# Warming TensorE by single fp32 products, and a down projection with standing weights for six of eight experts

## The chip, the core and the metric

One core of a Trainium2 chip runs the kernel. The metric is the device time of one execution in microseconds (us), the median of several runs. Its engines are TensorE (PE: products and transposes; PEld is its weight loading), VectorE (DVE), ScalarE (ACT), GpSimd (POOL) and SyncE (SP). Matrix products write PSUM, in eight banks; DMAs move data between SBUF and DRAM. Engines wait for each other by semaphores. PE's clock has two levels, 1.2 and 2.4 GHz; the profile gives the granted share.

## What is computed

A block on x (8, 16, 16, 128), so 2048 tokens of 128 channels, fp32: a linear attention with a residual, then a mixture of eight experts with a residual.

```python
x = x + conv_ref(_ln_c(x), w_qkv, q_gamma, q_beta, k_gamma, k_beta)   # heads of 16, q (k^T v) / n
t = _to_tokens(x)
t = t + ffn_ref(_ln_t(t), gate_w, gate_b, w1, b1, w2, b2)
...
# in ffn_ref: 8 experts, 2 per token, hidden 512
cap = int(CF * T / NE)                          # 307
probs = softmax(xf @ gate_w.T + gate_b)
topw, topi = top_k(probs, TOPK)
...
sel_w, sel_idx = top_k(wm.T, cap)               # each expert takes its 307 best tokens
xg = xf[sel_idx]
h = gelu(einsum('ecd,edh->ech', xg, w1) + b1[:, None, :], approximate=False)
out = einsum('ech,ehd->ecd', h, w2) + b2[:, None, :]
weighted = out * sel_w[..., None]
of = zeros((T, D)).at[sel_idx.reshape(-1)].add(weighted.reshape(-1, D))
```

## The kernel before, in words

Each engine has its own program, written out by hand in the order in which it runs; `wait_ge` and `then_inc` on named semaphores tie them together. There are four parts.

1. *Attention, 0 to 45 us.* The eight images go through a pipeline of steps over PE, ACT, DVE and POOL. SP loads x and the weights: after x come `gate_bias`, `b1_rows`, `w1_sb`, `w2_sb` and `b2_sb` (the biases b2 of all experts on every partition), then zeros are written to `parts`.
2. *Routing and thresholds, 45 to 76 us.* DVE computes the softmax and the two choices, and finds each expert's threshold, its 307th best weight, in nine rounds. In a round DVE compares (L729, `hits`), PE counts with 16 products (L1008, `ps_cnt`), DVE picks the digit (L743, L746). PE has time over in each round. It fills it with products on zeros, whose result nobody reads: `keep_warm` (L877) issues `times` bf16 products of `width` columns. There are 20 of 512 columns before the first round, 6 of 256 after each, 6 of 512 after the last and 10 of 512 after the running sums.
3. *Token lists, 76 to 90 us.* Of one-hot matrices PE makes the list of tokens of each expert (L1034 to L1054). POOL gathers the tokens' rows from `table` in DRAM by indirect DMAs: for each expert two of 128 rows (L436, `gather`), and for each pair of experts one with both tails of 51 rows (L441).
4. *Experts, 90 to 150 us.* 307 tokens are the chunks 128, 128 and 51. In the loop over e PE does
   - `up(e)`: four hidden blocks of 128, each w1 as weights and 307 tokens moving (L1072), into the banks `ps_h`;
   - `tokens_in(e + 1)`: three transposes of the gathered rows (L1066) into `ps_x`;
   - `down(e)`: three chunks (L1088), in each four products with the hidden values of 128 or 51 tokens as weights and w2 moving, 128 columns. They go by turns into the two banks `ps_ys`, so chunk n waits until chunk n - 2 is out (`y_ready`).

   A product in fp32 is two passes of PE, a transpose is one. ACT computes the gelu of each block with the bias b1 (L568), and copies `xgT` for experts 0 and 1 (L556). DVE copies the other `xgT` (L813), multiplies b2 by the tokens' weights ahead of time (`weigh_bias`, L825 and L827, into `wb2`) and takes each chunk out of PSUM by one instruction (L837, `tokens_out`): the product by the token's weight plus the weighted bias.

POOL scatters the rows to `parts` in DRAM (`put(e)`: one indirect DMA for each chunk of 128, L463, and one for the tails of a pair, L471; experts 6 and 7 have one each). All its transfers are one queue. The numbers of `GATHERS_AFTER` set it: ten gathers, put(0), three gathers (for expert 4 and the tails of 5), put(1), four gathers (5 and 6), put(2), three gathers (tails of 6 and 7, then 7), then put(3) to put(7). When the early puts are done SP loads the first half of `parts`, after put(7) the second; DVE adds both to the residual (L867, L871) and SP writes the result.

## Time and profile before

| | |
|---|---|
| median of 3 runs | 164.46 us (164.29 to 164.65) |
| profiled execution: its time | 163.72 us |
| its span, first to last instruction | 162.0 us |
| PE busy | 125.0 us (77%), 863 products or passes |
| PEld busy | 95.7 us (59%) |
| DVE busy | 86.7 us (54%), 324 instructions |
| ACT busy | 52.6 us (32%), 140 |
| POOL busy | 71.7 us (44%), 118 |
| down projection (L1088) | 192 passes, 26.7 us |
| up projection (L1072) | 64 passes, 22.8 us |
| `keep_warm` (L880) | 100 products, 21.2 us |
| instruction loads | 7 packets, 0.11 MB, 0.3% of the DMA engines |

Busy time is what an engine's instructions cover; a share of it doesn't say what sets the end. A row of the timeline gives the start in us from the span's beginning, the length, and in brackets how long the engine stood idle before and for whom. "issue" there names nobody.

### The profile page before, as it was taken

The numbers are of one execution on the slowest core, as the hardware profiler recorded it, in microseconds if no ns is written. First come the engines' busy times: TensorE is split into PE (matmuls) and PEld (weight loads), VectorE is DVE, ScalarE is ACT, GpSimd is POOL, SyncE is SP. The second block draws the span as 40 slices with busy tenths as digits, with TensorE's granted clock in tenths as the row PEclk, the third lists the DMA queues.
The fourth block names the chain that finished last, engine by engine and source line by source line (L and its number), as shares of the span: only waits on it lengthen the run. The fifth ranks groups of instructions, "written<-read, shape, count | busy, mean of one in ns | idle before, by whom it ended". The sixth has DMA issues, their size and how long they took to land.

```text
span 162.0 us, 2490 instructions
## 1 busy us (share of the span) xinstructions
PE 125.0 (77%) x863; PEld 95.7 (59%) x863; DVE 86.7 (54%) x324; ACT 52.6 (32%) x140; POOL 71.7 (44%) x118
## 2 busy tenths in 40 slices
PE   6899999998696564769985799983899799994000
PEld 3377999998642443545574468862668578873000
DVE  1567789766777888777863204321143234334442
ACT  3399777661289400000000242240040441450000
POOL 7405365456482060200048765777377244356100
PEclk9999999999959999999965569999569999999655
DMA  4679999300000008100001111112111010116497
GB/s 113 166 163 397 302 311 417 144 0 4 0 2 2 0 4 268 42 4 0 0 9 50 55 55 34 53 51 62 44 38 53 32 34 16 36 41 189 124 303 201
DMA packets 15596, 15.46 MB, mean 95 GB/s; under 512 B 1816, under 2 KB 12224, under 8 KB 15584
## 3 DMA queue, kind: packets, MB, share of 16 engines
q1 hardware_dynamic: 14240, 12.45, 24.7%
q0 software_dynamic: 1344, 2.86, 6.0%
q8 instruction: 7, 0.11, 0.3%
q14 instruction: 5, 0.04, 0.1%
HBM read 9.67 MB, written 5.64 MB: 94 GB/s over the span
## 4 chain that ended last, share of the span: by engine, by line
PE 48%; issue 26%; ACT 9%; DMA 7%; POOL 3%; SPq 2%; DVE 2%; POOLq 0%; another core or an unknown queue 0%; DVEq 0%
PE bank L1072 14%; PE bank L1088 14%; PE bank L903 4%; ACT rows L551 4%; DMA xb<-parts 3%; PE bank L930 2%; DMA vecs<-in_L_conv_k_beta_dram 2%; PE bank L943 2%; DMA parts<-y_tail,tail_rows 2%; PE bank L933 2%; PE bank L898 2%; PE bank L1066 2%; PE bank L916 1%; PE bank L960 1%; POOL parts L463 1%
## 5 line engine op out<-in xcount | busy, mean ns | idle before, releaser
L1088 PE MATMUL bank<-w_sb,hid 128*128 128x128 f32 (+1 forms) x192 | 26.7, 289 | 5.0 <-issue 4.8
L568 ACT ACTIVATE hid<-bank,b1T 128x307 f32<-128x307 f32 x32 | 16.3, 516 | 37.3 <-PE bank L1072 36.2
L1088 PEld LDWEIGHTS bank<-w_sb,hid 128*128 128x128 f32 (+1 forms) x192 | 22.7, 172 | 7.6 <-issue 5.5
L436 POOL DMA_INDIRECT kv<-table,index x16 | 16.5, 1032 | 20.5 <-DVE index L807 15.9
L463 POOL DMA_INDIRECT parts<-q_work,kv x16 | 15.9, 992 | 18.6 <-DVE q_work L837 10.8
L1072 PE MATMUL bank<-xgT,w_sb 128*128 128x307 f32 x64 | 22.8, 508 | 0.6 <-ACT xgT L556 0.6
L880 PE MATMUL bank<-warm_rhs 128*128 128x256 bf16 (+1 forms) x100 | 21.2, 356 | 1.4 <-POOL warm_rhs L355 1.4
L1072 PEld LDWEIGHTS bank<-xgT,w_sb 128*128 128x128 f32 x64 | 13.6, 224 | 6.8 <-issue 4.3
L837 DVE SCALAR_TENSOR_TENSOR q_work<-bank,kv,wb 128x128 f32<-128x128 f32 x16 | 5.6, 351 | 21.1 <-PE bank L1088 16.4
L1008 PE MATMUL bank<-hits,ones 128*128 128x56 bf16 (+1 forms) x144 | 7.8, 199 | 9.3 <-DVE hits L729 9.2
L880 PEld LDWEIGHTS bank<-warm_rhs 128*128 128x128 bf16 x100 | 9.5, 104 | 7.4 <-issue 2.7
L1008 PEld LDWEIGHTS bank<-hits,ones 128*128 128x128 bf16 x144 | 6.0, 97 | 12.7 <-DVE hits L729 9.7
L556 ACT ACTIVATE xgT<-bank 128x307 f32<-128x307 f32 x2 | 0.9, 426 | 36.1 <-issue 36.0
L415 POOL TENSOR_TENSOR att<-att,xb 128x256 f32<-128x256 f32 x8 | 5.8, 726 | 12.9 <-DVE xb L644 12.9
L813 DVE COPY xgT<-bank 128x307 f32<-128x307 f32 x6 | 2.9, 478 | 12.4 <-issue 12.4
L903 PE MATMUL bank<-w_c,xT 128*128 128x256 f32 x32 | 8.4, 386 | 0.3 <-ACT kv L538 0.3
L407 POOL TENSOR_TENSOR ksq<-kv,kq_rstd 128x256 f32<-128x256 f32 x8 | 5.0, 620 | 6.3 <-DVE kq_rstd L649 6.3
L903 PEld LDWEIGHTS bank<-w_c,xT 128*128 128x128 f32 x32 | 5.9, 190 | 1.9 <-ACT kv L538 1.1
L1034 PE MATMUL bank<-oh_tok,oh_maj 128*64 128x24 f16 (+1 forms) x48 | 6.0, 279 | 1.3 <-DVE oh_maj L785 1.3
L1034 PEld LDWEIGHTS bank<-oh_tok,oh_maj 128*64 128x64 f16 (+1 forms) x48 | 5.5, 195 | 1.9 <-DVE oh_maj L785 1.9
L1066 PEld LDWEIGHTS bank<-ident,kv 128*128 128x128 f32 (+1 forms) x24 | 3.7, 157 | 4.9 <-issue 3.9
L1066 PE MATMUL bank<-ident,kv 128*128 128x128 f32 (+1 forms) x24 | 5.2, 298 | 1.4 <-DMA kv<-table,index 1.4
(194 smaller groups left out, 235.6 us busy)
## 6 DMA issues: line engine op xcount, KB each, us to landing
w_sb<-in_L_ffn_w_dram SPq DMA_DIRECT2D x1, 2048.0 KB, 10.9
parts<-zeros SPq DMA_DIRECT2D x4, 512.0 KB, 7.2
table<-rows SPq DMA_DIRECT2D x1, 1152.0 KB, 5.4
x_sb<-parts SPq DMA_DIRECT2D x4, 256.0 KB, 3.9
xb<-parts SPq DMA_DIRECT2D x4, 256.0 KB, 3.8
out_dram<-att SPq DMA_DIRECT2D x4, 256.0 KB, 2.8
x_sb<-in_x_dram SPq DMA_DIRECT2D x1, 512.0 KB, 4.5
b_sb<-in_L_ffn_b_dram SPq DMA_DIRECT2D x1, 512.0 KB, 18.0
```

The costliest lines, as they stand in the source:

```text
L415: pool.tensor_tensor(x1[:, img(b), :], att[:, img(b), :], xb[:, img(b), :], ALU.add).then_inc(x1_ready, 1)
L436: pool.indirect_dma_start(out=xg_chunk(e, c), out_offset=None, in_=table, in_offset=bass.IndirectOffsetOnAxis(ap=index[:, index_at(e, c):i ...
L463: pool.indirect_dma_start(out=parts, out_offset=bass.IndirectOffsetOnAxis(ap=xg_rows[:, e // 2, at, C + E + e:C + E + e + 1], axis=0), in_ ...
L551: act.activation(rows[:, t, 0:C], x1[:, t, :], ACT.Identity, bias=shift2[:, t:t + 1], scale=rstd2[:, t:t + 1]).then_inc(x2_ready, 1)
L568: act.activation(hid[:, e % 2, c, :], ps_h[c][:, 0:CAP], ACT.Gelu, bias=b1T[:, e * HC + c:e * HC + c + 1]).then_inc(h_ready, 1)
L880: pe.matmul(bank[:, 0:width], warm_rhs[:, 0:P], warm_rhs[:, 0:width], start=True, stop=True)
L903: ins = pe.matmul(ps_kv[:, i * 2 * C:(i + 1) * 2 * C], xT[:, t * P:(t + 1) * P], w_c[:, C:3 * C], start=True, stop=True)
L1008: ins = pe.matmul(ps_cnt[:, 0:n * E], ones16[:, :], hits[:, r % 2, 0:n, t, :], start=(t == 0), stop=(t == NT - 1))
L1034: ins = pe.matmul(ps_grids[g][0:MAJ * m, 0:CM * m], majors[:, :, t], minors[:, :, t], start=(t == 0), stop=(t == NT - 1))
L1066: ins = pe.transpose(ps_x[:, at:at + n], xg_chunk(e, c)[:, 0:C], ident[own, own])
L1072: pe.matmul(ps_h[c][:, 0:CAP], w1_sb[:, e, c * P:(c + 1) * P], xgT[:, e % 2, :], start=True, stop=True).then_inc(h_done, 1)
L1088: ins = pe.matmul(ps_ys[(NC * e + k) % 2][y_at:y_at + n, 0:C], hid[:, e % 2, c, at:at + n], w2_sb[:, e, c, :], start=(c == 0), stop=(c == ...
```

## The change

Two parts, and what hangs on them.

*Warming.* A new `keep_warm_long` multiplies the fp32 tile `zeros` by itself. Before the rounds there are 6 of 512 columns instead of 20 bf16 ones, after each round 1 of 384 instead of 6 of 256, after the last 1 of 512 instead of 6, after the running sums 2 instead of 10. The other calls of `keep_warm` stay.

*Down projection.* `TURNED` is 6. For experts 0 to 5 the weights w2 stand and the 307 tokens move: four products into bank 5 give the output with channels on the partitions (`down_turned`). ACT takes it out and adds b2 as a bias per partition (`yT`). PE turns it back by three products on the identity into bank 6 (`turn`; a chunk that lands on partitions 64 and up is an ordinary product, not a transpose), one expert later: `turn(e - 1)` stands between `tokens_in(e + 1)` and `down(e)`. DVE multiplies by the token's weight, both chunks of 128 in one instruction and the tail in a second (`turned_out`). For experts 6 and 7 all stays as it was. The rows of b2 are loaded and turned with those of b1; only two experts' b2 is spread over the partitions.

```diff
+    TURNED = E - 2
...
+        yT = sb("yT", [C, 2, CAP])
...
+        ps_yT = banks[5]
+        ps_turned = banks[6]
...
+        def written(e, c):
+            if e < TURNED:
+                return 2 * e + (1 if c < LAST else 2)
+            return 2 * TURNED + NC * (e - TURNED) + c + 1
...
+            sp.dma_start(b_rows[0:E * HC, :], b1.rearrange("e (c p) -> (e c) p", p=P)).then_inc(b_in, 16)
+            sp.dma_start(b_rows[E * HC:E * HC + E, :], b2).then_inc(b_in, 16)
...
-                         b2.rearrange("e c -> (e c)").partition_broadcast(P)).then_inc(b_in, 16)
+                         b2[TURNED:E, :].rearrange("e c -> (e c)").partition_broadcast(P)).then_inc(b_in, 16)
...
-                    pool.wait_ge(y_ready, NC * e + c + 1)
+                    pool.wait_ge(y_ready, written(e, c))
...
+                if e < TURNED:
+                    act.wait_ge(yT_done, e + 1)
+                    if e >= 2:
+                        act.wait_ge(y_done, e - 1)
+                    act.activation(yT[:, e % 2, :], ps_yT[:, 0:CAP], ACT.Identity,
+                                   bias=bT[:, E * HC + e:E * HC + e + 1]).then_inc(yT_ready, 1)
...
+            def turned_out(e):
+                at, last = e % 2 * HALF, CHUNKS[LAST][1]
+                slot_of, to = tail_of(e)
+                dve.wait_ge(y_done, e + 1)
+                dve.tensor_tensor(y[:, e, :, :], ps_turned[:, 0:LAST * C].rearrange("p (n c) -> p n c", c=C),
+                                  main_weight(e), ALU.mult).then_inc(y_ready, 1)
+                dve.tensor_scalar(y_tail[to:to + last, slot_of, :], ps_turned[at:at + last, LAST * C:NC * C],
+                                  xg_chunk(e, LAST)[:, C + e:C + e + 1], None, ALU.mult).then_inc(y_ready, 1)
...
-            weigh_bias(0)
-            tokens_out(0)
-            weigh_bias(1)
+            tail_to(0)
             for e in range(1, E):
+                tail_to(e)
+                if e >= TURNED:
+                    weigh_bias(e)
                 if e + 1 < E:
                     tokens_in(e + 1)
-                tokens_out(e)
-                if e + 1 < E:
-                    weigh_bias(e + 1)
+                if e - 1 < TURNED:
+                    turned_out(e - 1)
+                if e >= TURNED:
+                    tokens_out(e)
...
+            def keep_warm_long(bank, times, width=512):
+                for _ in range(times):
+                    pe.matmul(bank[:, 0:width], zeros[:, 0:P], zeros[:, 0:width], start=True, stop=True)
...
-            keep_warm(ps_kv, 20)
+            pe.wait_ge(zeros_ready, 1)
+            keep_warm_long(ps_kv, 6)
...
-                keep_warm(ps_kv, 6, 2 * P)
-            keep_warm(ps_kv, 6)
+                keep_warm_long(ps_kv, 1, 3 * P)
+            keep_warm_long(ps_kv, 1)
...
-            keep_warm(ps_kv, 10)
+            keep_warm_long(ps_kv, 2)
...
+            def down_turned(e):
+                if e >= 1:
+                    pe.wait_ge(yT_ready, e)
+                for c in range(HC):
+                    pe.wait_ge(h_ready, HC * e + c + 1)
+                    ins = pe.matmul(ps_yT[:, 0:CAP], w2_sb[:, e, c, :], hid[:, e % 2, c, :],
+                                    start=(c == 0), stop=(c == HC - 1))
+                ins.then_inc(yT_done, 1)
+
+            def turn(e):
+                pe.wait_ge(yT_ready, e + 1)
+                if e >= 1:
+                    pe.wait_ge(y_ready, 2 * e)
+                for k, (at, n) in enumerate(CHUNKS):
+                    y_at = e % 2 * HALF if k == LAST else 0
+                    block = ps_turned[y_at:y_at + n, k * C:(k + 1) * C]
+                    if y_at == 0:
+                        ins = pe.transpose(block, yT[:, e % 2, at:at + n], ident[:, :])
+                    else:
+                        ins = pe.matmul(block, yT[:, e % 2, at:at + n], ident[:, :], start=True, stop=True)
+                ins.then_inc(y_done, 1)
...
+                if 1 <= e <= TURNED:
+                    turn(e - 1)
                 down(e)
```

PE, expert 1 of the loop, before: `up(1)`, `tokens_in(2)`, `down(1)`. The up projection is L1072 (`xgT` its tokens), the input transposes L1066 (`kv` the gathered rows), the down projection L1088.

```order
L1072 MATMUL bank<-xgT,w_sb 128x307 [waits h_ready,xgT_ready]
L1072 MATMUL bank<-xgT,w_sb 128x307 [waits h_ready] x3
L1066 MATMUL bank<-ident,kv 128x128 [waits xgT_ready,pair_gathered1,gathered2]
L1066 MATMUL bank<-ident,kv 128x128
L1066 MATMUL bank<-ident,kv 128x51
L1088 MATMUL bank<-w_sb,hid 128x128 [waits h_ready,y_ready]
L1088 MATMUL bank<-w_sb,hid 128x128 [waits h_ready] x3
L1088 MATMUL bank<-w_sb,hid 128x128 [waits y_ready]
L1088 MATMUL bank<-w_sb,hid 128x128 x3
L1088 MATMUL bank<-w_sb,hid 51x128 [waits y_ready]
L1088 MATMUL bank<-w_sb,hid 51x128 x3
```

And in the change, where the up projection is L1111, the input transposes L1105, `down_turned` L1124 and `turn` L1136:

```order
L1111 MATMUL bank<-xgT,w_sb 128x307 [waits h_ready,xgT_ready]
L1111 MATMUL bank<-xgT,w_sb 128x307 [waits h_ready] x3
L1105 MATMUL bank<-ident,kv 128x128 [waits xgT_ready,pair_gathered1,gathered2]
L1105 MATMUL bank<-ident,kv 128x128
L1105 MATMUL bank<-ident,kv 128x51
L1136 MATMUL bank<-ident,yT 128x128 [waits yT_ready]
L1136 MATMUL bank<-ident,yT 128x128
L1136 MATMUL bank<-ident,yT 51x128
L1124 MATMUL bank<-hid,w_sb 128x307 [waits h_ready,yT_ready]
L1124 MATMUL bank<-hid,w_sb 128x307 [waits h_ready] x3
```

Twelve products with three waits for `y_ready` became three products on the identity, which belong to expert 0, and four products of 307 columns with one wait for `yT_ready`.

ACT, experts 0 and 1, before: the copy of `xgT` is L556, the gelus L568.

```order
L556 ACTIVATE xgT<-bank 128x307 [waits xgT_done]
L568 ACTIVATE hid<-bank,b1T 128x307 [waits h_done] x4
L556 ACTIVATE xgT<-bank 128x307 [waits xgT_done]
L568 ACTIVATE hid<-bank,b1T 128x307 [waits h_done] x4
L568 ACTIVATE hid<-bank,b1T 128x307 [waits y_done,h_done]
L568 ACTIVATE hid<-bank,b1T 128x307 [waits h_done] x3
```

In the change the copy is L568, the gelus L580 and the evacuation of `yT` L586:

```order
L568 ACTIVATE xgT<-bank 128x307 [waits xgT_done]
L580 ACTIVATE hid<-bank,bT 128x307 [waits h_done] x4
L586 ACTIVATE yT<-bank,bT 128x307 [waits yT_done]
L568 ACTIVATE xgT<-bank 128x307 [waits xgT_done]
L580 ACTIVATE hid<-bank,bT 128x307 [waits h_done] x4
L586 ACTIVATE yT<-bank,bT 128x307 [waits yT_done]
L580 ACTIVATE hid<-bank,bT 128x307 [waits yT_done,h_done]
L580 ACTIVATE hid<-bank,bT 128x307 [waits h_done] x3
```

The evacuation of expert 0's output, which waits for `yT_done`, now stands ahead of the copy of expert 1's tokens.

## Rows read from the trace of the kernel before

**Rows 1.** The page, the chain that ended last: shares of the span

```profile
PE 48%; issue 26%; ACT 9%; DMA 7%; POOL 3%; SPq 2%; DVE 2%; POOLq 0%; another core or an unknown queue 0%; DVEq 0%
PE bank L1072 14%; PE bank L1088 14%; PE bank L903 4%; ACT rows L551 4%; DMA xb<-parts 3%; PE bank L930 2%; DMA vecs<-in_L_conv_k_beta_dram 2%; PE bank L943 2%; DMA parts<-y_tail,tail_rows 2%; PE bank L933 2%; PE bank L898 2%; PE bank L1066 2%; PE bank L916 1%; PE bank L960 1%; POOL parts L463 1%
```

**Rows 2.** PE's waits: who waited for whom, us in total, times, longest

```profile
PE bank L1008 <- DVE hits L729: 9.2, 10, 2.1
```

**Rows 3.** Stretches: us, busy of PE, PEld, DVE, ACT, POOL, granted clock

```profile
54.30:75.10 20.80, 13.56 (x191) 9.83 (x189) 16.81 (x61) 0.33 (x2) 3.68 (x7) 1.00 0.21 62
...
104.88:115.93 11.05, 7.07 (x36) 5.39 (x36) 2.01 (x6) 1.96 (x4) 7.84 (x9) 0.87 0.19 55
115.93:123.58 7.65, 7.65 (x36) 5.71 (x35) 2.76 (x8) 2.07 (x4) 4.54 (x5) 0.74 0.14 42
123.58:131.06 7.48, 6.42 (x36) 4.76 (x35) 2.21 (x7) 1.96 (x4) 3.36 (x4) 1.00 0.08 27
131.06:136.73 5.67, 5.67 (x36) 4.53 (x36) 2.38 (x7) 2.07 (x4) 1.94 (x2) 1.00 0.07 25
```

**Rows 4.** The chain in order of time: start us, us, what

```profile
96.30 2.99 PE bank L1088 x24
...
131.13 2.27 PE bank L1072 x8
133.40 0.41 PE bank L1066 x3
...
146.30 0.27 issue
```

**Rows 5.** PE's timeline: start us, us, engine, line, what, count, idle before it

```profile
45.43 5.89 PE L880 MATMUL bank<-warm_rhs 128*128 128x512 bf16 x20
...
89.69 0.94 PE L1066 MATMUL bank<-ident,kv 128*128 128x128 f32 x3 [1.39 <-DMA kv<-table,index]
...
107.05 0.57 PE L1066 MATMUL bank<-ident,kv 128*128 128x128 f32 x3
...
109.23 1.38 PE L1088 MATMUL bank<-w_sb,hid 128*128 128x128 f32 x10 [0.54 <-issue]
114.05 1.95 PE L1088 MATMUL bank<-w_sb,hid 128*51 128x128 f32 x8 [3.44 <-issue]
```

**Rows 6.** DVE's timeline, experts 0 to 3

```profile
99.86 0.42 DVE L825 TENSOR_TENSOR wb<-b_sb,kv 128x256 f32<-128x256 f32 x1
...
105.52 0.41 DVE L825 TENSOR_TENSOR wb<-b_sb,kv 128x256 f32<-128x256 f32 x1
...
110.14 0.48 DVE L813 COPY xgT<-bank 128x307 f32<-128x307 f32 x1 [3.87 <-issue]
113.65 0.35 DVE L837 SCALAR_TENSOR_TENSOR q_work<-bank,kv,wb 128x128 f32<-128x128 f32 x1 [3.03 <-remote]
117.19 0.35 DVE L837 SCALAR_TENSOR_TENSOR q_work<-bank,kv,wb 128x128 f32<-128x128 f32 x1 [3.19 <-PE bank L1088]
```

**Rows 7.** POOL's groups, 97 to 151 us: busy us, mean ns, idle before

```profile
L463 POOL DMA_INDIRECT parts<-q_work,kv x16 | 15.9, 992 | 18.6 <-DVE q_work L837 10.8 <-issue 5.0 <-DVE y_tail L837 2.9
L436 POOL DMA_INDIRECT kv<-table,index x8 | 7.7, 960 | 2.4 <-issue 2.4
```

**Rows 8.** POOL's timeline in the expert phase

```profile
86.83 0.94 POOL L441 DMA_INDIRECT kv<-table,index  x1 [0.30 <-issue]
...
98.65 0.99 POOL L463 DMA_INDIRECT parts<-q_work,kv  x1 [2.14 <-issue]
...
104.00 0.94 POOL L441 DMA_INDIRECT kv<-table,index  x1 [0.30 <-issue]
105.25 1.00 POOL L463 DMA_INDIRECT parts<-q_work,kv  x1 [0.30 <-issue]
...
149.11 1.13 POOL L471 DMA_INDIRECT parts<-y_tail,tail_rows  x1 [0.30 <-issue]
```

**Rows 9.** ACT's timeline, the first copy of the expert phase

```profile
90.67 0.43 ACT L556 ACTIVATE xgT<-bank 128x307 f32<-128x307 f32 x1 [36.03 <-issue]
```

More of the change, by code:

```diff
@@ L89, in build @@
         gate_bias = sb("gate_bias", [P, E])
-        b1_rows = sb("b1_rows", [E * HC, P])
-        b2_sb = sb("b2_sb", [P, E, C])
+        b_rows = sb("b_rows", [E * HC + E, P])
+        b2_sb = sb("b2_sb", [P, E - TURNED, C])
         w1_sb = sb("w1_sb", [C, E, HID])
@@ L158, in build @@
         gateT = sb("gateT", [C, E])
-        b1T = sb("b1T", [P, E * HC])
+        bT = sb("bT", [P, E * HC + E])
         logit = sb("logit", [P, NT, E])
@@ L1092, in down @@
             def down(e):
-                for k in range(NC):
-                    down_chunk(e, k)
+                if e < TURNED:
+                    down_turned(e)
+                else:
+                    for k in range(NC):
+                        down_chunk(e, k)
             find_tokens(0, 0, NT // 2)
```

55 lines of the change are left out of this document (30 added, 25 removed).

## The prediction

> **What bounds the kernel now.** I read the views in this order: the chain that ended last, PE's waits, the stretches of the expert phase, then the timelines of TensorE (PE), VectorE (DVE), ScalarE (ACT) and GpSimd (POOL) there.
>
> The chain is half PE, and the two expert products alone (L1072, L1088) are 28% of the span [rows 1]. The 26% of "issue" is mostly one piece: from 54.6 to 90.7 us the chain sits behind ACT's first copy and can't be followed. There DVE leads: PE waits for its comparisons ten times, 9.2 us in all [rows 2]. So in the first 90 us I expect warming products, which stand in those waits, to be worth nothing either way.
>
> In the expert phase an undisturbed expert takes 5.67 us of PE with no gap [rows 3]: 2.27 for eight passes of the up projection (307 columns), 0.41 for three transposes, 2.99 for 24 passes of the down projection (128 columns) [rows 4]. Three experts are longer: 11.05, 7.65 and 7.48 us [rows 3]. Against 5.67 that is 5.38 + 1.98 + 1.81 = 9.17 us lost.
>
> Where do they go? In expert 2 PE stops 0.54 and 3.44 us [rows 5], in expert 4 it stands 7.48 - 6.42 = 1.06 us in small pieces; the rest is mostly the low clock that follows the long stop (0.87 and 0.74 of full in the first two of these stretches) [rows 3]. The long stop has an odd cause. PE's transposes for expert 3 are issued by 107.05 and end at about 107.6 [rows 5], yet DVE, which waits for nothing else, copies them at 110.14. The first output chunk is multiplied by 109.7 and DVE takes it at 113.65; the second by 110.6, taken at 117.19 [rows 6]. PE then stops because the buffer of chunk 0 isn't emptied. So PE's answers reach the others 2.5 to 6.5 us late there. I don't know why. What the rows do show is when: from the first scatter that POOL issues straight behind gathers, 0.30 us apart (105.25 [rows 8]; the same again in experts 3 and 4), until POOL's queue runs dry. Where scatters come alone, after 129, nothing is late.
>
> **The change, part by part.**
>
> *Warming.* 90 bf16 products (20 of 512 columns, 54 of 256, 16 of 512) become 18 fp32 products, two passes each. Behind each stands one of the ten waits for DVE, 0.9 us on average [rows 2]: cost 0, cover 9.2 us. A fp32 pass of 307 columns takes 2.27/8 = 0.28 us [rows 4], so one of 512 some 0.45: the first block is 12 x 0.45 = 5.4 us at the full clock and at most 10.8 at half of it, where 5.89 stood [rows 5] ahead of a wait of 2.1 [rows 2]. The upper end would hold the first comparison up by 10.8 - 8.0 = 2.8 us; I take 0, nearest to the block it replaces, whose 5.89 us were a mixture of both levels too.
>
> *Loads.* One more small DMA on SP, and 384 KB less of b2. Both lie under the first 45 us, in which nothing waits for them: 0.
>
> *Down projection of experts 0 to 5.* 24 passes of 128 columns (2.99) become 8 of 307 columns, the same shape as the up projection: 2.27. That saves 0.72 in each of six: 4.32 us. The turning back adds three products on the identity in stages 1 to 6, as the input transposes 0.41 [rows 4]: 6 x 0.41 = 2.46. For the three odd experts the tail is an ordinary fp32 product, two passes of 2.99/24 = 0.125 instead of one of 0.11: 3 x 0.14 = 0.4. Net 4.32 - 2.46 - 0.4 = **-1.46 us**.
>
> *ACT's queue.* The evacuation with the bias (307 columns, Identity) is priced as the copy of the same shape, 0.43 [rows 9]; bounds: 0 and twice that, as its neighbours hide it. Five of six are hidden: PE doesn't need one until 2.7 us later, and ACT has over 3 us free in every stage. The first isn't hidden. ACT's order is gelu(0), evacuation of yT(0), copy of xgT(1); the old order had no evacuation between. So up(1) can't begin before down(0) has ended, plus 0.43, plus 0.43, plus hand-overs (0.14 from ACT's end at 91.10 to PE's start): PE stands about 1.0 us. **+1.0 us**.
>
> *DVE.* The two weighings on SBUF inputs (0.42 and 0.3 to 0.4 us) vanish for six experts, three evacuations of 0.35 become one of 256 elements (0.41) and one tail. DVE has idle time before each of them, so 0 on the path. A row bears on POOL too: the weighing at 105.52 took 0.41 beside a scatter of 1.00 issued at 105.25; at 99.86 it took 0.42, and scatters take 0.99 on average [rows 6 to 8]. Neither held the other up. The Trainium skill, SBUF — State Buffer, "Who interferes with whom", speaks of a lock: a DVE instruction with two SBUF inputs contends with a GpSimd instruction that reads SBUF, and one waits for the whole of the other. By that rule taking six of them away would give POOL up to 6 x 0.4 = 2.5 us; by the rows it gives 0, which is what the sum has.
>
> *The answers that come late.* In experts 0 to 5 an output no longer needs three answers through two banks before PE may go on: it needs one, and that one has a whole stage to arrive. The stop of 3.44 us hung on that loop alone: **-3.44 us**. In its place PE still waits for the gelus, which wait for PE's answers: what that cost in expert 4, **+1.06 us**, I count once more, because scatters follow gathers for longer now. Bounds: with no such wait nothing is added and the low clock after the stop goes as well (to -9.17 in all); if the state merely moves, nothing is gained.
>
> *POOL.* Its order of transfers is the same, but expert e's scatters are ready one stage later. The first scatter stood at 98.65 [rows 8]. Now down(0) begins at 96.30 as before [rows 4] and ends by 98.6; then come the stop of 1.0, up(1) 2.27, transposes 0.41, turning 0.41, DVE 0.41 and a hand-over to POOL of 0.27 [rows 4]: 103.4. From there stand 21 scatters and 10 gathers, at 0.99 + 0.30 and 0.96 + 0.30 [rows 7]: 27.1 + 12.6 = 39.7 us, so POOL can't end before 143.1. It ended at 149.11 + 1.13 = 150.24 before [rows 8]. This floor allows at most -7.1 us. Gathers stand behind scatters in that queue: the one that carries the tails of experts 6 and 7 is through POOL at 122.5 and lands some 1.9 us later (the third gather ended at 87.77, PE began at 89.69 [rows 5, 8]), 124.4, while PE at full pace would ask for it at about 99.6 + 4 x 5.4 + 2.27 = 123.5. At the forecast's pace PE comes later, so it costs 0.
>
> *Sum.* 163.72 (span 162.0 and 1.72 around it) - 1.46 + 1.0 - 3.44 + 1.06 = 160.9. The median of the runs lies 0.74 above the profiled one: **161.6 us**.
>
> **The rivals.**
>
> *Nothing is late any more* (17%). For it: one answer a stage instead of three. Against: POOL is busier than before. PE would run 9 us faster than it did and run into POOL's floor: 164.46 - 7.1 = 157.4.
>
> *The lateness stays as it was and only moves* (17%): it may have nothing to do with the number of answers. Left are -1.46 + 1.0: 164.0, on the edge of no change.
>
> *POOL's mixed queue keeps PE's answers late for longer; slower* (23%). Before, answers were late from about 106.2 to 117.2 and from 123.7 to 127.8 (where DVE and ACT begin late in their timelines), 15.1 us, at 9.17/15.1 = 0.61 us lost in each. Now the scatters of expert 1 stand straight behind gathers at 103.4 + 6.4 = 109.8, and the queue need not run dry until those of expert 3 are out: 3 + 4 + 2 + 3 + 3 transfers, 19.1 us, till 128.9. With 1.9 of landing 21.0 us are late: 12.8 lost, 3.6 more than before: 164.46 + 3.6 - 0.46 = 167.6. It decides if PE is held up as a share of that time, not by the loop through two banks. For it: both late stretches coincide with such a queue. Against: expert 4 lost only 1.06 us in gaps.
>
> *The fp32 products on zeros don't hold the clock* (5%). The stretch of the rounds shows PE at 1.00 with bf16, 13.56 us busy of 20.8 [rows 3]. PE's share of a round, its products for the comparison, is about half of that, 7 us, and would double at half the clock, less where columns don't set its pace: 3 to 7 us, of which I take 3: 167.5. Against: the expert phase runs fp32 at 1.00 [rows 3].
>
> That the change does less than it says isn't a case: the order of PE shows the 72 products of six experts turned into 24 plus 18.
>
> **How the numbers follow.** A measurement of this kernel can tell about 0.2% (0.33 us) from no change. The forecast (38%) reaches from 160 to 163.3 by its own bounds; with the first rival and a third of the second it is faster: 61%. The rest of the second is the same: 11%. The last two are slower: 28%. Most of the chance has one sign, and the range, 157.4 to 167.0, reaches to the floor below and almost to the slower cases; what is left out is under 2 in 10.
>
> **What would show it.** Right: no PE gap of over 1 us in experts 1 to 5; stages of 5.4 us where nothing is late; one gap of about 1.0 us ahead of up(1), named after ACT; first scatter at about 103; POOL nearly unbroken from there to 129 or later; granted clock 1.00 from 55 to 75 us. Wrong: DVE or ACT starting microseconds after PE's product ended, over more than 15 us; a PE wait for a gather; a clock below 1.00 in the rounds; or a first comparison that waits for the long warming.

## The result, and the profile after

| | before | after |
|---|---|---|
| median | 164.38 us (4 runs, 163.14 to 164.65) | 167.96 us (4 runs, 167.09 to 169.53) |
| profiled execution, its span | 163.72 us, 162.0 us | 167.72 us, 166.0 us |
| PE's last product ends | 147.73 us | 149.05 us |
| last scatter issued | 149.11 us [rows 8] | 153.66 us |

The change makes the kernel slower: the ratio is 1.025, 95% interval 1.018 to 1.033. The forecast was 161.6 us; the time is above its range, which ended at 167.0. A ratio compares executions on one chip, and only those in the faster of two states that this program shows; a median is over all of them.

Of the page of the kernel after, PE's line and the chain. PE is as busy as before, with 733 entries in place of 863; the chain has less "issue" than before [rows 1] and POOL's transfers in it.

```profile
PE 125.5 (76%) x733; PEld 89.7 (54%) x734; DVE 80.2 (48%) x306; ACT 55.6 (34%) x146; POOL 71.5 (43%) x118
...
PE 51%; DVE 12%; issue 11%; POOL 9%; DMA 9%; ACT 3%; SPq 2%; POOLq 0%; DVEq 0%
```

PE's timeline after: start us, us, engine, line, what, count, idle before it. L1111 is the up projection, L1105 the transposes of the tokens, L1124 the turned down projection, L1136 and L1138 the turning back, L1152 the down projection of the last two experts.

```profile
99.46 2.34 PE L1111 MATMUL bank<-xgT,w_sb 128*128 128x307 f32 x8 [0.92 <-ACT xgT L568]
...
112.14 0.57 PE L1105 MATMUL bank<-ident,kv 128*128 128x128 f32 x3
...
113.03 2.24 PE L1124 MATMUL bank<-hid,w_sb 128*128 128x307 f32 x8
115.25 2.33 PE L1111 MATMUL bank<-xgT,w_sb 128*128 128x307 f32 x8
118.10 0.63 PE L1105 MATMUL bank<-ident,kv 128*128 128x128 f32 x3 [0.51 <-DMA kv<-table,index]
125.90 0.69 PE L1136 MATMUL bank<-ident,yT 128*128 128x128 f32 x2 [7.17 <-issue]
...
127.42 4.77 PE L1124 MATMUL bank<-hid,w_sb 128*128 128x307 f32 x8 [0.23 <-issue]
...
145.89 3.16 PE L1152 MATMUL bank<-w_sb,hid 128*128 128x128 f32 x24
```

The first row is the forecast stop behind ACT, 0.92 us. Expert 4's stage starts at 115.25 and goes well for 3 us; then PE stands 7.17 us in front of the turning back of expert 3, and the eight passes at 127.42 take 4.77 us where eight took 2.24 or 2.34 us in stages 1 to 3.

The stretches show the same: us, busy of PE, PEld, DVE, ACT, POOL, granted clock.

```profile
99.46:104.60 5.14, 5.14 (x22) 3.75 (x23) 1.21 (x4) 2.07 (x4) 0.62 (x1) 1.00 0.02 3
...
110.07:115.25 5.18, 5.18 (x23) 3.45 (x21) 0.48 (x1) 2.58 (x5) 3.93 (x4) 1.00 0.17 52
115.25:127.42 12.17, 4.26 (x17) 2.34 (x16) 0.73 (x3) 1.03 (x2) 7.72 (x8) 0.80 0.19 53
127.42:132.80 5.38, 5.38 (x10) 3.29 (x11) 1.23 (x4) 1.85 (x4) 2.79 (x3) 0.50 0.07 24
...
143.50:149.10 5.60, 5.55 (x35) 4.30 (x33) 1.55 (x5) 2.07 (x4) 4.08 (x5) 1.00 0.14 48
```

Stages 1 to 3 take 5.14 to 5.47 us, about the 5.4 of the prediction. From the start of up(4) to that of up(6) (137.43) pass 22.18 us; where nothing is late the same two stages take 10.50 (below). So 11.7 us are lost here, where before all three long stretches together lost 9.17 [rows 3]. The clock is part of it: granted 0.80 of full in the stretch with the stop, 0.50 in the next, after the long idle.

ACT's timeline, what it does with PE's answers:

```profile
112.57 0.52 ACT L580 ACTIVATE hid<-bank,bT 128x307 f32<-128x307 f32 x1 [0.23 <-issue]
125.33 0.52 ACT L586 ACTIVATE yT<-bank,bT 128x307 f32<-128x307 f32 x1 [12.25 <-remote]
...
128.18 1.33 ACT L580 ACTIVATE hid<-bank,bT 128x307 f32<-128x307 f32 x3 [0.91 <-remote]
```

and DVE's:

```profile
108.00 0.42 DVE L855 TENSOR_TENSOR q_work<-bank,kv 128x256 f32<-128x256 f32 x1 [0.24 <-issue]
...
114.72 0.48 DVE L831 COPY xgT<-bank 128x307 f32<-128x307 f32 x1 [5.85 <-remote]
116.86 0.43 DVE L855 TENSOR_TENSOR q_work<-bank,kv 128x256 f32<-128x256 f32 x1 [1.66 <-remote]
...
128.31 0.48 DVE L831 COPY xgT<-bank 128x307 f32<-128x307 f32 x1 [10.72 <-remote]
...
150.16 0.35 DVE L868 SCALAR_TENSOR_TENSOR q_work<-bank,kv,wb 128x128 f32<-128x128 f32 x1 [2.44 <-PE bank L1152]
153.03 0.35 DVE L868 SCALAR_TENSOR_TENSOR y_tail<-bank,kv,wb 51x128 f32<-51x128 f32 x1 [2.52 <-remote]
```

"Done" is here the end that the profile gives a product. These ends are modelled, so a trace can't tell an answer that comes late from a product that ended late; the text calls both a late answer. The product of expert 3 (L1124 at 113.03, 2.24 us) was done at 115.27. ACT, which had nothing else to do, takes it at 125.33, 10 us later. PE's transposes of 112.14 (done 112.7) are copied by DVE at 114.72, those of 118.10 (done 118.73) at 128.31. At the end the same happens again: PE's last product ends at 149.05, DVE takes the last but one chunk at 150.16 and the tail at 153.03, where before its last chunk was taken 0.04 us after PE (147.77 after 147.73). So the last scatter is issued 4.55 us later: 1.32 by PE's end, 3.94 by the late answer, less 0.71 in which POOL before had still another scatter to issue. Behind the last scatter the program is 0.55 us shorter (12.34 us left of the span against 12.89), which makes the 4.0 us between the two profiled executions.

POOL's timeline. An unbroken run is here a row of transfers that POOL issues 0.30 us apart. From the first to the second row below there are 17; from the fourth on seven, up to 150.07.

```profile
103.98 0.99 POOL L475 DMA_INDIRECT parts<-q_work,kv  x1 [6.68 <-DVE y_tail L857]
...
124.42 0.94 POOL L448 DMA_INDIRECT kv<-table,index  x1 [0.30 <-issue]
129.40 0.99 POOL L475 DMA_INDIRECT parts<-q_work,kv  x1 [4.04 <-DVE q_work L855]
...
141.53 0.97 POOL L475 DMA_INDIRECT parts<-q_work,kv  x1 [2.76 <-DVE q_work L855]
...
153.66 1.22 POOL L483 DMA_INDIRECT parts<-y_tail,tail_rows  x1 [1.91 <-DVE y_tail L868]
```

POOL's unbroken run ends at 125.36; ACT gets its answer at 125.33 and PE goes on at 125.90.

In the kernel before, the run that begins at 98.65 has 12 transfers; two rows of its timeline show how it breaks up behind them:

```profile
114.28 0.99 POOL L463 DMA_INDIRECT parts<-q_work,kv  x1 [0.42 <-issue]
117.82 0.98 POOL L463 DMA_INDIRECT parts<-q_work,kv  x1 [2.55 <-DVE y_tail L837]
```

There POOL had to wait for expert 2's second chunk. After the change both chunks of expert 2 are ready (DVE at 116.86) before their turn comes at 119.27, and the run goes on through them and the three gathers behind.

### The profile page after: what moved, and what is told of

It is laid out like the page before. It is cut to its first block, busy times and chain, and to the rows that moved or that the text cites. A ratio compares the mean times of both kernels' runs of the same rounds, so it can differ in the third digit from the quotient of the medians.

```text
span 166.0 us, 2222 instructions
## 1 busy us (share of the span) xinstructions
PE 125.5 (76%) x733; PEld 89.7 (54%) x734; DVE 80.2 (48%) x306; ACT 55.6 (34%) x146; POOL 71.5 (43%) x118
## 4 chain that ended last, share of the span: by engine, by line
PE 51%; DVE 12%; issue 11%; POOL 9%; DMA 9%; ACT 3%; SPq 2%; POOLq 0%; DVEq 0%
PE bank L1111 8%; PE bank L918 6%; PE bank L1124 6%; PE bank L1047 5%; PE bank L1152 4%; PE bank L941 4%; POOL kv L448 4%; POOL parts L475 3%; DMA xb<-parts 3%; DMA kv<-table,index 3%; DVE hits L747 2%; PE bank L968 2%; DMA vecs<-in_L_conv_k_beta_dram 2%; PE bank L981 2%; PE bank L1105 2%
## 5 line engine op out<-in xcount | busy, mean ns | idle before, releaser
L475 POOL DMA_INDIRECT parts<-q_work,kv x16 | 15.9, 994 | 20.9 <-DVE y_tail L857 10.0
L1111 PE MATMUL bank<-xgT,w_sb 128*128 128x307 f32 x64 | 20.3, 465 | 1.5 <-ACT xgT L568 0.9
L918 PE MATMUL bank<-zeros 128*128 128x512 f32 (+1 forms) x36 | 20.2, 684 | 0.0
L580 ACT ACTIVATE hid<-bank,bT 128x307 f32<-128x307 f32 x32 | 16.3, 517 | 10.2 <-PE bank L1111 7.2
L1111 PEld LDWEIGHTS bank<-xgT,w_sb 128*128 128x128 f32 x64 | 13.2, 212 | 7.7 <-issue 3.0
L1124 PE MATMUL bank<-hid,w_sb 128*128 128x307 f32 x48 | 16.2, 482 | 0.2 <-issue 0.2
L1047 PEld LDWEIGHTS bank<-hits,ones 128*128 128x128 bf16 x144 | 6.8, 106 | 12.3 <-DVE hits L747 11.4
L568 ACT ACTIVATE xgT<-bank 128x307 f32<-128x307 f32 x2 | 0.8, 422 | 36.3 <-issue 36.3
L1124 PEld LDWEIGHTS bank<-hid,w_sb 128*128 128x128 f32 x48 | 9.5, 212 | 4.5 <-issue 1.5
L586 ACT ACTIVATE yT<-bank,bT 128x307 f32<-128x307 f32 x6 | 3.1, 517 | 24.9 <-remote 12.2
L918 PEld LDWEIGHTS bank<-zeros 128*128 128x128 f32 x36 | 7.4, 235 | 4.8 <-issue 4.5
L1136 PE MATMUL bank<-ident,yT 128*128 128x128 f32 (+1 forms) x15 | 3.2, 315 | 7.2 <-issue 7.2
L483 POOL DMA_INDIRECT parts<-y_tail,tail_rows x5 | 5.0, 1003 | 3.1 <-DVE y_tail L868 1.9
```

Of the source, the lines that this page charges most:

```text
L475: pool.indirect_dma_start(out=parts, out_offset=bass.IndirectOffsetOnAxis(ap=xg_rows[:, e // 2, at, C + E + e:C + E + e + 1], axis=0), in_ ...
L580: act.activation(hid[:, e % 2, c, :], ps_h[c][:, 0:CAP], ACT.Gelu, bias=bT[:, e * HC + c:e * HC + c + 1]).then_inc(h_ready, 1)
L918: pe.matmul(bank[:, 0:width], zeros[:, 0:P], zeros[:, 0:width], start=True, stop=True)
L1047: ins = pe.matmul(ps_cnt[:, 0:n * E], ones16[:, :], hits[:, r % 2, 0:n, t, :], start=(t == 0), stop=(t == NT - 1))
L1111: pe.matmul(ps_h[c][:, 0:CAP], w1_sb[:, e, c * P:(c + 1) * P], xgT[:, e % 2, :], start=True, stop=True).then_inc(h_done, 1)
L1124: ins = pe.matmul(ps_yT[:, 0:CAP], w2_sb[:, e, c, :], hid[:, e % 2, c, :], start=(c == 0), stop=(c == HC - 1))
```

## The experiments

Each run changes one thing; a few change two, and say so. The question was why PE's answers (the semaphores that say a product is done) reach ACT and DVE up to 10 us late. The theories at the start: **S**, the scatters do it (their writes to DRAM); **M**, it takes gathers and scatters in turn in POOL's queue; **Q**, a long run of POOL's indirect transfers without a break does it, of whatever kind. Later came **N**: it begins at about the 16th transfer of the program and the breaks don't matter. A rival to all of them was that the warming, or the turned projection by itself, costs the time. The runs stand in the order of the argument; each comes with its ratio to the kernel before on the same chip.

**The warming alone.** The kernel before, its `keep_warm` replaced:

```diff
-            keep_warm(ps_kv, 20)
+            pe.wait_ge(zeros_ready, 1)
+            keep_warm_long(ps_kv, 6)
...
-                keep_warm(ps_kv, 6, 2 * P)
-            keep_warm(ps_kv, 6)
+                keep_warm_long(ps_kv, 1, 3 * P)
+            keep_warm_long(ps_kv, 1)
...
-            keep_warm(ps_kv, 10)
+            keep_warm_long(ps_kv, 2)
```

> The kernel before with the long fp32 warming alone. If half of the loss is the warming (the clock fell for one stretch inside the rounds and the expert phase began 0.7 us later in the changed kernel): granted clock below 1.00 somewhere between 50 and 70 us, first input transposes at about 90.3 instead of 89.7, time 0.6 to 1.0 us above the kernel before, about 165.2. If warming costs nothing: the same as before, 164.4. If the warming caused the long stop of PE too (through the clock or the later start): 167 to 168.

Measured: 165.19 us, ratio 1.001 (0.997 to 1.005). The warming costs nothing that can be measured, and of the three expectations the second holds. From 54.3 to 75.1 us the granted clock is 0.92 in this profile and 0.84 in that of the kernel after, against 1.00 before [rows 3]. But it is 0.92 with the old warming in the next run too, and 0.84 in the kernel before with six breaks, so these profiles don't tell the warmings apart. The first gather of the lists stands between 83.05 and 85.3 us with either warming, but for the run with six early gathers. There are late answers in expert 2 here as well, and ACT takes the four products of that up projection at 108.28, 109.71, 111.14 and 112.56.

**The turned projection alone.** The kernel after with the warming of before (the diff above, reversed).

> The changed kernel with the old bf16 warming. If the turned down projection carries the rest: 167.1, with one PE stop of 5 to 7 us in experts 3 or 4 and a stop of 0.9 us ahead of the second up projection. If the loss came from the warming alone: 164 or below, and no stop over 4 us.

Measured: 167.93 us, ratio 1.018 (1.010 to 1.026). PE stops 6.48 us behind ACT's yT at 125.67, as the first expectation had it. The loss sits in this half of the change.

**All gathers before the first scatter.**

```diff
-    GATHERS_AFTER = (10, 3, 4, 3)
+    GATHERS_AFTER = (20,)
```

> The changed kernel, with all 20 gathers ahead of the first scatter (GATHERS_AFTER = (20,)), so gathers and scatters are never mixed. Theory M (PE's answers are late only where scatters stand straight behind gathers): the switch happens once, at about 109 us, when POOL has five scatters ready; late answers there for some microseconds at most, then none; PE's end near 140 and the time 157 to 161. Theory Q (any POOL queue without a pause for over 7 us makes PE's answers late, whatever is in it): answers late from before 105 us, in the middle of the gathers, and the time at or above the changed kernel's, 168 or more. Theory S (it takes scatters in an unbroken queue, mixed or not): answers in time until about 112, late from then on as long as scatters follow each other; 164 to 168.

Measured: 166.82 us, ratio 1.013 (1.006 to 1.020). PE's row with the stop, and POOL's last gather and first scatter:

```profile
112.49 4.46 PE L1111 MATMUL bank<-xgT,w_sb 128*128 128x307 f32 x8 [4.13 <-DVE xgT L831]
```

```profile
109.11 0.94 POOL L448 DMA_INDIRECT kv<-table,index  x1 [0.30 <-issue]
114.61 1.00 POOL L475 DMA_INDIRECT parts<-q_work,kv  x1 [4.56 <-DVE y_tail L857]
```

The answers are late in a run of gathers alone, before any scatter; PE goes on 2.4 us after that run has ended (110.05). From 115 to 140 us, where the scatters go out two or three at a time, nothing is late. That speaks against S and M, though the time lies in the range of S; Q had the place right (the first late answer is due at 102.7, about the fifteenth gather) and the time too high. At the end answers are late again, behind seven scatters in a row that end at 149.08. PE's last product is done at 148.03, and DVE takes it here:

```profile
152.00 0.35 DVE L868 SCALAR_TENSOR_TENSOR y_tail<-bank,kv,wb 51x128 f32<-51x128 f32 x1 [2.53 <-remote]
```

**No scatters at all.** Each scatter of the kernel after is replaced by a gather of 128 rows into memory that nobody reads, so the experts' part of the output is left out.

```diff
-                        out=parts, out_offset=bass.IndirectOffsetOnAxis(
-                            ap=xg_rows[:, e // 2, at, C + E + e:C + E + e + 1], axis=0),
-                        in_=y[:, e, c, :], in_offset=None).then_inc(done, 16)
+                        out=dump[dumped[0]], out_offset=None, in_=table,
+                        in_offset=bass.IndirectOffsetOnAxis(ap=index[:, index_at(e, c):index_at(e, c) + 1], axis=0)).then_inc(done, 16)
...
```

The scatters of the tails are replaced in the same way.

> The changed kernel with each of the 21 scatters replaced by a gather of 128 rows into a tile nobody reads, so the experts' part is left out of the output; POOL issues the same number of indirect DMAs behind the same waits. Theory S or M (scatters needed): no PE stop over 1 us in the expert phase but the one ahead of the second up projection, PE's last product by 140 us, span about 155. Theory Q (an unbroken queue is enough): the long stop stays, 5 to 8 us at about 118 to 126 us, span about 166.

Measured: 169.07 us (one run).

```profile
127.05 0.69 PE L1141 MATMUL bank<-ident,yT 128*128 128x128 f32 x2 [8.87 <-ACT yT L591]
```

The long stop is there without one scatter. S and M fall.

**Six more gathers, early.** The kernel before, with six gathers of table rows where POOL waits for the lists.

```diff
             pool.wait_ge(pool_started, 16)
+            for k in range(6):
+                pool.indirect_dma_start(out=unread[:, k, :], out_offset=None, in_=table,
+                                        in_offset=bass.IndirectOffsetOnAxis(ap=first_rows[:, 0:1], axis=0)
+                                        ).then_inc(pool_started, 16)
```

> The kernel before, with six more gathers of 128 table rows into unread space, right behind the first gather at about 67 to 76 us, where POOL waits for the lists. Theory N (a count from the start of POOL's queue, about 16 transfers): TensorE's answers come late six transfers sooner, from 95 to 99 us in place of 106, more stages fall into the spell, 166 to 169 us. Theory Q (the unbroken run): the extra transfers end over 5 us before the first gather of the lists, onset stays at 105 to 107 us, time as before, 164 to 165.5 us.

Measured: 167.23 us, ratio 1.017 (1.007 to 1.028). The time is what N gave, but the trace shows another reason. DVE's timeline in the rounds, where it waits for PE's count:

```profile
73.05 0.22 DVE L748 SCALAR_TENSOR_TENSOR best<-bank,cand 128x56 f32<-128x56 f32 x1 [1.76 <-PE bank L1013]
...
77.42 0.28 DVE L748 SCALAR_TENSOR_TENSOR best<-bank,cand 128x120 f32<-128x120 f32 x1 [2.21 <-PE bank L1013]
```

In the kernel before the idle in front of these two is 0.37 and 0.48 us. Six gathers from 68.84 to 76.51, nothing else on POOL, and two answers of PE come 1.4 and 1.5 us after its counts are done (71.62 and 75.91), where before they came 0.03 us after; the first is due while the third of them is out; the lists start 3.2 us later (86.23 against 83.05) and the kernel ends later by about that. In the expert phase the first late answers stand at 107 to 108 us, as before, and not at 95 to 99. N's count from the start falls, and Q's expectation of "as before" was wrong too, since it took six transfers for too few. It is the smallest case of the effect: a short run of plain gathers delays PE's answers. But the number of transfers isn't all. The kernel before issues its first ten gathers of the lists from 83.05 to 96.51, also 0.30 us apart, and beside the tenth PE's transposes are done at 96.30 and ACT copies them at once:

```profile
96.33 0.43 ACT L556 ACTIVATE xgT<-bank 128x307 f32<-128x307 f32 x1
```

Why six gathers do here what ten don't do there wasn't tested.

**Breaks in POOL's queue.** After every transfer this is called; where its number is in `PAUSES`, POOL waits until that transfer has landed. The gathers are spread otherwise as well.

```diff
-    GATHERS_AFTER = (10, 3, 4, 3)
+    GATHERS_AFTER = (13, 2, 3, 2)
+    PAUSES = (5, 10, 15, 20, 25, 30)
...
+            def sent(done):
+                on_queue[0] += 1
+                sent_to[id(done)] = sent_to.get(id(done), 0) + 1
+                if on_queue[0] in PAUSES:
+                    pool.wait_ge(done, 16 * sent_to[id(done)])
```

> The changed kernel; POOL waits for the landing of its own transfer after the 5th, 10th, 15th, 20th, 25th and 30th on its queue (counted from the first gather of the lists), and 13 gathers are issued before the first scatter in place of 10, then 2, 3, 2. Theory Q (TensorE's answers come late after a long unbroken run of POOL's indirect transfers, and catch up when the run breaks): no spell before 140 us, the 7.17 us stop and the second low clock before it are gone, last scatter at 150 to 151; 157 to 161 us. Theory N (late from about the 16th transfer on, whatever breaks there are): onset at 105 to 108 us, a stop of 3 to 7 us remains, 165 to 169 us. A third, that the breaks only delay the gathers of experts 4 to 7: stops of TensorE on the gathers, 167 us or more.

Measured: 160.82 us, ratio 0.977 (0.968 to 0.985). PE's waits from 95 us on (us in total, times, longest) have one line left:

```profile
PE bank L1124 <- ACT xgT L581: 0.9, 1, 0.9
```

POOL's timeline, one of the six breaks and the last scatter:

```profile
93.10 0.94 POOL L457 DMA_INDIRECT kv<-table,index  x1 [1.83 <-DMA kv<-table,index]
...
144.91 0.90 POOL L495 DMA_INDIRECT parts<-y_tail,tail_rows  x1 [0.30 <-issue]
```

Six waits of 1.5 to 2.4 us on POOL, and PE ends 11.5 us sooner, at 137.56 in place of 149.05: stages 1 to 5 take 5.0 to 5.5 us, and the granted clock is 1.00 from 99.8 to 137.5 us. Now POOL is behind: from 132.25 on it sends 11 scatters that have been ready, and the last goes out at 144.91. That is what Q gave, with the last scatter 5 us sooner than it expected; N and the third theory fall.

**The same breaks in the kernel before.** The same edit.

> The kernel before with the same breaks in POOL's queue (after the 5th, 10th, 15th, 20th, 25th and 30th transfer) and gathers 13, 2, 3, 2. Theory Q: the spells of 106 to 117 and 123.65 to 129 us are gone, with the stops at two banks of y (3.44 us by the sum of the prediction) and the late gelus (2.27 and 0.41), 159 to 162 us. Theory N: spells stay, 164 to 167 us.

Measured: 160.6 us, ratio 0.972 (0.961 to 0.982). The view of PE's waits is empty from 95 us on, and the stages take 5.66 us but for one of 6.35, in which a gelu begins 0.90 us late (108.86). That is again what Q gave. So the edit takes 2.8% off the kernel before as well, and then the two kernels take the same time: both wait for POOL at the end (last scatter 146.27 here). How much of it is the other spread of the gathers wasn't run apart for the kernel before.

**The other spread without the breaks.** Only `GATHERS_AFTER = (13, 2, 3, 2)`.

> The changed kernel with gathers 13, 2, 3, 2 as in the last runs, but without any wait of POOL for a landing. If the breaks in POOL's queue are what took the 7 us away, the spell is back: one or more stops of TensorE of 4 to 8 us between 108 and 130 us, 165 to 169 us. If the other spread of the gathers did it, no spell, 158 to 161 us (POOL has 8 to 9 us less to wait than with the breaks).

Measured: 163.32 us, ratio 0.991 (0.986 to 0.996). The spell is back, but smaller:

```profile
119.92 0.78 PE L1124 MATMUL bank<-hid,w_sb 128*128 128x307 f32 x2 [0.65 <-issue]
122.04 2.80 PE L1124 MATMUL bank<-hid,w_sb 128*128 128x307 f32 x4 [1.33 <-ACT hid L580]
```

```profile
121.18 0.96 POOL L448 DMA_INDIRECT kv<-table,index  x1 [0.30 <-issue]
```

Neither expectation held; the time lies between them, and the longest stop is 1.33 us. The unbroken run has 14 transfers and ends at 122.14 in place of 17 and 125.36; PE's last stop ends at 122.04. By the ratios the spread is worth 3.3% of the kernel after, the breaks 1.5% more.

**ACT's order.** The kernel after; ACT copies expert 1's tokens ahead of its product of expert 0.

```diff
-                if e == 1:
-                    tokens_in(1)
...
+                if e == 0:
+                    tokens_in(1)
                 if e < TURNED:
```

> The changed kernel with one edit: ScalarE copies expert 1's tokens ahead of its product of expert 0. The stop of 0.92 us ahead of the first stage of expert 1 goes. If the late spell is tied to POOL's queue, expert 0's scatter moves by 0 to 0.5 us, the spell and its 7 us stay: 167.0 to 168.0 us, with a stop of 6.5 to 7.5 us on the product of expert 3. If the spell is tied to TensorE's own work, it moves by the same 0.9 us: 167.0 us.

Measured: 165.2 us (10 runs, 163.4 to 166.7), ratio 1.002 (0.995 to 1.009). Both expectations were too high. The stop of 0.92 is gone, and with it more: against the 1.025 of the change some 2.3%. POOL's run has its 17 transfers and ends at 124.64, 0.72 us sooner. But the late answers now cost PE stops of 0.72, 0.69, 0.68 and 1.41 us (and a gather 0.75) in place of one of 7.17:

```profile
118.69 0.44 PE L1136 MATMUL bank<-ident,yT 128*128 128x128 f32 x2 [0.72 <-issue]
...
126.44 1.39 PE L1124 MATMUL bank<-hid,w_sb 128*128 128x307 f32 x2 [1.41 <-issue]
```

So the same 17 transfers cost the two stages 9.2 us here and 11.7 in the kernel after; why wasn't found. The trace shows how the answers come. PE's row of the up projection of expert 4, and ACT's rows for the product of expert 3 (L586) and for the four products of that up projection (L578):

```profile
114.37 2.23 PE L1111 MATMUL bank<-xgT,w_sb 128*128 128x307 f32 x8
```

```profile
118.12 0.52 ACT L586 ACTIVATE yT<-bank,bT 128x307 f32<-128x307 f32 x1 [6.00 <-remote]
119.51 0.52 ACT L578 ACTIVATE hid<-bank,bT 128x307 f32<-128x307 f32 x1 [0.88 <-remote]
121.64 0.52 ACT L578 ACTIVATE hid<-bank,bT 128x307 f32<-128x307 f32 x1 [1.61 <-remote]
123.06 0.52 ACT L578 ACTIVATE hid<-bank,bT 128x307 f32<-128x307 f32 x1 [0.90 <-remote]
125.87 0.52 ACT L578 ACTIVATE hid<-bank,bT 128x307 f32<-128x307 f32 x1 [2.29 <-remote]
```

All four products were done by 116.60, and ACT takes them one by one, 1.4 to 2.8 us apart, three of them while POOL's run is still going. So the answers aren't simply held until the run ends: they are passed on late and singly, and each further one adds to the delay (4.6 us for the first, over 9 for the last).

**Fewer breaks.** The kernel after with ACT's order, gathers 13, 2, 3, 2 and `PAUSES = (10, 16, 22, 28)`, and the same with `(13, 20, 27)`.

> The changed kernel, ScalarE's copy of expert 1's tokens ahead of its product of expert 0, gathers 13, 2, 3, 2, and POOL waits for its own landing after the 10th, 16th, 22nd and 28th transfer (four waits of 1.5 to 1.8 us in place of six). If runs of six transfers still end before the answers come late: TensorE's work ends 0.9 us sooner than with six breaks (136.7 us), the last scatter is issued at 141 to 142 us in place of 144.9: 157 to 159 us. If six are too many: a stop of 1 to 5 us, 161 to 165 us.

> As the run with four breaks, but with three, after the 13th, 20th and 27th transfer (runs of 13, 7 and 7). If only TensorE's stage of 99 us and later is hurt by a long run, and seven transfers are short enough: last scatter at 140 to 141 us, 156 to 158 us. If the run of 13 or of 7 is too long: stops of TensorE of 1 to 7 us from 102 us on, 161 to 167 us.

Measured, four breaks: 158.2 us, ratio 0.962 (0.953 to 0.970), the fastest of the study, 6.2% under the kernel after by the two ratios. PE's last product, and what becomes of it on DVE and POOL:

```profile
133.32 3.16 PE L1165 MATMUL bank<-w_sb,hid 128*128 128x128 f32 x24
```

```profile
143.32 0.36 DVE L881 SCALAR_TENSOR_TENSOR y_tail<-bank,kv,wb 51x128 f32<-51x128 f32 x1 [5.26 <-remote]
```

```profile
143.96 0.90 POOL L495 DMA_INDIRECT parts<-y_tail,tail_rows  x1 [1.27 <-DVE y_tail L881]
```

The time is in the range of the first expectation; the last scatter is 2 us later than it said. PE has no stop and is done at 136.5. Its last answer still comes 6.8 us late, in the unbroken run from 127.76 on; POOL waits 1.27 us for it.

Three breaks: 160.34 us, ratio 0.972 (0.957 to 0.986). Two gelus are late at 103.7 and 105.1, at the end of the run of 13, and PE stops four times, 3.4 us, from 136 us on, in the run of 11 from 127.16. Here the second expectation came nearer, by the long runs: those of 7 in the middle cost PE no stop, though one answer behind the second of them is 1.1 us late (DVE at 126.51).

**The kernel before with four breaks.**

> The kernel before (down projection with tokens standing, short bf16 warming), with the four breaks and gathers 13, 2, 3, 2 of the run at 158.2 us. What the change itself brings once the answers are in time: with six breaks, the kernels before and after stood at 160.6 and 160.8 us, both held up by POOL's queue at the end (last scatter 146.3 and 144.9 us). If POOL's queue bounds both with four breaks too: 157.5 to 159.5 us. If TensorE's longer stages (5.66 us against 5.2 to 5.5) come to the end of the chain again: TensorE ends at 140 to 141 us against 136.5, last scatter at 144.5 to 146, 159.5 to 161 us. If runs of six are too long for the four products into two banks of y: stops on them, 161 to 164 us.

Measured: 161.2 us, ratio 0.985 (0.976 to 0.994). PE's waits name a late output and a late gelu:

```profile
117.69 1.08 PE L1101 MATMUL bank<-w_sb,hid 128*51 128x128 f32 x8 [0.80 <-DVE q_work L850]
...
141.65 4.68 PE L1101 MATMUL bank<-w_sb,hid 128*128 128x128 f32 x24 [3.32 <-ACT hid L581]
```

The old down projection meets the lateness in a run of six (0.80 us, 117.69) and in the long one at the end (3.32, 141.65); the turned one with ACT's order has no stop. That is the third of the expectations. Between the two ratios lie 2.4%, so with these four breaks the change and ACT's order are worth something together; with six breaks and no change of ACT's order there was nothing between the kernels. How much of it is the turned projection wasn't run apart.

The six kernels that hold the change, from their profiles; "two stages" is from the start of up(4) to that of up(6):

| kernel | longest run with scatters, its end | two stages | PE ends | last scatter | median |
|---|---|---|---|---|---|
| after | 17, 125.36 | 22.18 | 149.05 | 153.66 | 167.96 |
| ACT's order | 17, 124.64 | 19.69 | 145.67 | 150.16 | 165.2 |
| other spread | 14, 122.14 | 17.30 | 143.54 | 148.03 | 163.32 |
| three breaks, ACT's order | 11 at the end | 10.50 | 143.03 | 146.26 | 160.34 |
| six breaks | 11 at the end | 10.50 | 137.56 | 144.91 | 160.82 |
| four breaks, ACT's order | 12 at the end | 10.50 | 136.48 | 143.96 | 158.2 |

## Why the prediction was wrong

**Wrong: the term of -3.44 us.** It rested on the sentence that an output now needs one answer "and that one has a whole stage to arrive". The lateness was read as a delay of some us for each answer, which one answer with a slack of a stage would hide. The trace before allowed that reading because there the longest unbroken run had 12 transfers. In the kernel after, with 17, one answer comes 10 us late, and a stage is 5.4; a slack of one stage is then too little. That the run of transfers is the cause is shown by the breaks: without them (the other spread alone) there are stops again, with them there are none but ACT's. The +1.06 for late gelus was too small by the same error: with the forecast 9.17 - 3.44 + 1.06 = 6.79 us are lost, measured are 11.7, which is 4.9 more.

**Missing from the sum** was the end. The last chunks' answers came late as well (150.16 and 153.03), behind seven scatters in a row. The change itself puts them there: the rows of expert 5 now come one stage later and those of expert 6 don't, so the scatters of both and the first of expert 7 follow each other from 141.53 to 150.07. The run with all gathers first shows it too (152.00 for a product done at 148.03), though nothing was late there for 25 us before. The late last answer is 3.94 of the us by which the last scatter moved, against 1.32 by PE's own end; after the 0.71 and 0.55 us of above, 2.7 of it are left in the time.

**Right.** The warming costs 0: shown by a run of its own. Its first block took 7.94 us where 5.4 to 10.8 was given (with 0.28 us for 307 columns, 512 take 0.47, so 5.7 to 11.4 was meant), and the first comparison begins at 53.55, 0.13 us later than before. ACT's queue: 0.92 us named after ACT ahead of up(1), forecast 1.0. The first scatter: 103.98, forecast 103.4. POOL nearly unbroken from there: until 125.36, forecast 128.9. The gather with the tails of experts 6 and 7 cost nothing, as forecast. The 0.51 us at 118.10 are another gather, of expert 5's own rows, issued at 115.51 behind expert 1's scatters, which the sum didn't price. POOL's transfers kept their length (L475 994 ns on average, 992 before [rows 7]) with the twelve weighings of DVE gone, so the term 0 held. The prediction set it against the lock of the Trainium skill (SBUF — State Buffer, "Who interferes with whom"). But the same section says that a `tensor_tensor` with both inputs in SBUF takes only the read interface of the shared pair, and infers that generating descriptors needs the write interface; the rows agree with that.

**Right in sign, too small:** the -1.46 us. Stages 1 to 3 took 5.14 to 5.47 us. With four breaks and ACT's order, where PE has no stop, it takes 39.82 us from down(0) (96.66) to its end (136.48); before, the undisturbed pieces add up to 2.99 + 6 x 5.67 + 5.33 = 42.34. So the instructions save 2.5 us (the moved order of ACT is part of that kernel). In the kernel after the gain was lost to waits for late answers. The profiled execution was forecast at 160.9 us and took 167.72: of the 6.8 between them 4.9 are the two late stages and 2.7 the end, less 0.7 or 0.8 of cheaper work on PE.

Of the signs of being wrong, three came: ACT and DVE that start late, a PE wait for a gather, and a clock below 1.00 in the rounds (0.84), which cost nothing.

**The slower rival came nearest**, at 167.6 us for a measured 167.96, and it had the direction right: POOL's queue keeps the answers late for longer. The closeness of its number is partly luck. It lost 12.8 us where 11.7 were lost, and had nothing for the 2.7 us at the end. Its condition was too narrow: not scatters behind gathers, but any indirect transfers of POOL. It had 23% because "expert 4 lost only 1.06 us in gaps" counted against it; that run had 7 transfers. Its fixed share of lost time, 0.61 us for each us of lateness, doesn't hold either, since the same 17 transfers cost 11.7 and 9.2 us in two kernels.

## What to carry to other kernels

Look for consumers that start microseconds after their producer ended while they have nothing else to do, and lay POOL's queue beside it: here the cure was to leave gaps in a long row of indirect transfers, at 1.5 to 2.4 us of POOL each. With the other spread of the gathers it took 2.8% off the kernel before and 4.7% off the one after. A cheaper piece of PE's work brings nothing while its answers are held back, and a step that moves POOL's transfers closer together can take back more than it gives. Price such a state by the run in which it appears and by where it ends, not by the delay that one trace happens to show.

## What the runs showed of the hardware

PE's answers reached other engines up to 10 us late (115.27 to 125.33) while POOL issued indirect DMAs 0.30 us apart. The longest delays ended between 0.7 us before the row of transfers did (the turned projection alone: 125.10 and 125.84) and 3.0 us after it (the end of the kernel after: 153.03 and 150.07). Late answers came singly, 1.4 us apart (108.28, 109.71, 111.14, 112.56 with the warming alone) or 1.4 to 2.8 (ACT's order). The effect needs no scatters (8.87 us of stop without one) and is there with six gathers and an otherwise quiet POOL (1.4 and 1.5 us).

After a gap, mixed rows of five, six and seven transfers in the middle of the expert phase passed mostly without harm (the longest stop there is 0.80 us), while from about the seventh or eighth on answers were late in the kernels before and after. In rows of gathers alone the first late answer came at the twelfth to fifteenth, and the first ten were harmless; in the row of six early gathers one was late at the third. So no length is safe by these runs, and the length isn't the whole condition. What holds the answers back was not found: no run took POOL's work of issuing apart from the moving of the data, and the modelled ends leave open whether the product or its semaphore is late.

The granted clock fell to half after the long stops and added to them: 4.77 us for eight passes that take 2.24.

The Trainium skill, SBUF — State Buffer, "Who interferes with whom", says that a DMA never contends with a compute engine, and that PE and ACT never wait on anyone. As a rule on SBUF's ports this is not contradicted: PE's own products kept their length beside the transfers (2.23 and 2.24 us at 110.07 and 113.03). Taken as a promise for a pipeline it fails here: PE's next product waited 7.17 us for ACT, and ACT for PE's own answer.
